# A selective scan with a shared feed-forward network: joined slot order, tanh gates, row shift on GpSimd, logits copied by ScalarE

## The chip, the cores and the metric

The kernel runs on 1 core of one Trainium2 chip. The metric is the device time of one execution in microseconds (us), the median of several runs; lower is better.

## What is computed

Two residual blocks on `x` of 4 x 512 tokens with 512 features. The first is a selective scan (Mamba's cross form: the context goes in, the normalised `x` is the gate `z`); the second is a mixture of 16 experts of which each token takes two, beside one shared expert of twice the width that every token takes.

```python
x = x + xattn(ctx, layernorm(x))            # first block
#   u = silu(conv(ctx @ in_proj)); dt, B, C from u
#   state = state * exp(dt * A) + (dt * u) * B ; y = sum_n state * C
#   y = (y + D * u) * silu(z)
n = layernorm(x)
logits = n @ gate_w.T ; top 2 of softmax    # routing, 16 experts
x = x + sum over the 2 experts (silu(g) * u) @ w_down * weight
      + (silu(g_s) * u_s) @ shared_down     # shared expert, 2 x 352 wide
```

## The kernel before, in words

The program is written out by hand for five engines, each with its own list of instructions, and semaphores between them. It has four stages: a prelude that makes `u`, `dt`, `B`, `C` and `silu(z)` for each of the 4 batches and stores them; the scan; a stretch that finishes the shared expert and computes the routing tables; and the routed experts.

**The scan stage** has 16 slots, one for each batch `b` and quarter `q` of the 512 channels. A slot has 16 steps `n`, one for each state. In a step ScalarE makes the decay `exp(dt * A)` in one of three PSUM banks (`decay`, L838), VectorE scans it with `dbu` (`scan`, L1226), and the result times `C` is made by VectorE (`times_c`, L1237, 12 states, tile `gs`, a ring of six) or by GpSimd (`times_c`, L1057, states 1, 5, 9 and 13, tile `g_p`, a ring of two). GpSimd makes `dbu` for four states at a time (L1043) for the slot after the one that VectorE scans: a group can be written when the scan has left it. TensorE adds the products up turned, in the bank `Y` (`y_sum`, L546, in the order `ORDER`).

**Between these steps lies the shared expert.** While batch `b` is scanned, slot `(b, q)` also treats tile `j = (b-1)*4+q` of 128 tokens of the batch before, and the next one. The constants at L41 to L51 say after which step `n` each piece of it stands on its engine. On TensorE `slot` (L625) takes ten early pieces of the next tile (`PE_AT`: eight halves of the four products of `rows_in`, L600, each two matrix products of 352 columns, then two turns, L608), six late pieces of the present tile (`LATE_AT`: the down projection, L618, each one product of 512 columns), the router (L579, into the first 16 columns of bank `YO`) and the turn of the normalised rows (L571). ScalarE applies the gate (`gate`, L851, Silu of a 128x352 half `c`), copies the turned hidden rows (`hT_copy`, L856 and L857), makes the normalised rows (`xn`, L863) and copies them turned (`xnT_copy`, L868). VectorE makes the hidden rows (`hidden`, L1276, gate times up), the statistics (`stats`, L1256 to L1261), the row shift minus mean times `rstd` (`norm`, L1266), copies the logits out of `YO` (`lg_copy`, L1270) and adds the down product to the rows (`add_shared`, L1281). GpSimd only raises the variance to the power of -1/2 (`rstd`, L1061).

The waits that matter: the second product into a gate's bank waits for `sg_ready` (the gate has been read); `hidden` waits for the gate and for the up product; the first down piece waits until the logits have left `YO`; `add_shared` waits for the last down piece; TensorE's first early piece of a slot waits for `hT_copy`. The scan stage is followed by `whole` for the tiles that are left, and by the routing in VectorE's list (L1347 to L1427).

The constants that set the places before:

```python
RSTD_AFTER = 2
LATE_AT = (0, 0, 0, 0, 0, 2, 3, 4, 4, 4, 6, 6, 6, 6, 6, 6, 6)
XN_TURN_AT, ROUTER_AT = (12, 9), 1
TAKE_AT, LOGITS_AT, GATED_AT, HIDDEN_AT, STATS_AT, NORM_AT, ADD_AT = 2, 4, 4, (12, 15), (10, 1), (12, 5), 13
```

## Time and profile before

| what | value |
|---|---|
| time, median of 3 runs (lowest to highest) | 1181.41 us (1180.92 to 1182.24) |
| the profiled execution: its own time | 1183.43 us |
| its span | 1181.7 us |
| busy: TensorE, VectorE, ScalarE, GpSimd | 937.7, 851.1, 534.8, 717.6 us |
| granted TensorE clock, mean | 0.877 of full speed |
| scan stage, from the first scan to the last product read | 166.9 to 701 us |
| from there to the last routing table | 701 to 798 us |
| routed experts | from 798 us |

The durations below are from the profiled execution, whose own time lies 2.0 us above the median. The shares of busy time are means over stages with different limits; the rows are therefore read inside one slot.

### The profile page before, as it was taken

The numbers are of one execution on the slowest core, as the hardware profiler recorded it, in microseconds if no ns is written. First come the engines' busy times: TensorE is split into PE (matmuls) and PEld (weight loads), VectorE is DVE, ScalarE is ACT, GpSimd is POOL, SyncE is SP. The second block draws the span as 40 slices with busy tenths as digits, with TensorE's granted clock in tenths as the row PEclk, the third lists the DMA queues.
The fourth block names the chain that finished last, engine by engine and source line by source line (L and its number), as shares of the span: only waits on it lengthen the run. The fifth ranks groups of instructions, "written<-read, shape, count | busy, mean of one in ns | idle before, by whom it ended". The sixth has DMA issues, their size and how long they took to land.

```text
span 1181.7 us, 16742 instructions
## 1 busy us (share of the span) xinstructions
PE 937.7 (79%) x4328; PEld 677.0 (57%) x4329; DVE 851.1 (72%) x1398; ACT 534.8 (45%) x918; POOL 717.6 (61%) x445
## 2 busy tenths in 40 slices
PE   5777414667788887888778898996999899988993
PEld 1222103455455555555555555564999899887893
DVE  4467457998889878888799861377879888888200
ACT  3677623444445453554454432201455455443551
POOL 0222359997777766767677510001789788876783
PEclk9777656578899888889888898998999999999997
DMA  8637230155122732146222013003586776776332
GB/s 278 256 140 286 109 125 18 54 187 201 57 72 63 276 125 70 44 136 232 86 71 71 27 53 128 18 19 109 130 223 165 200 208 173 215 193 161 66 66 36
DMA packets 69589, 152.03 MB, mean 129 GB/s; under 512 B 7200, under 2 KB 23584, under 8 KB 63920
## 3 DMA queue, kind: packets, MB, share of 16 engines
q1 hardware_dynamic: 59024, 126.97, 30.9%
q0 software_dynamic: 10528, 24.65, 11.4%
q8 instruction: 13, 0.21, 0.1%
q14 instruction: 24, 0.20, 0.1%
HBM read 112.80 MB, written 38.80 MB: 128 GB/s over the span
## 4 chain that ended last, share of the span: by engine, by line
DVE 27%; PE 25%; issue 15%; DMA 8%; ACT 5%; POOL 4%; DVEq 1%; ACTq 0%; SPq 0%; POOLq 0%
PE bank L600 10%; DMA e_gu<-in_wgu 6%; DVE e_gu_lo L1454 5%; DVE gs L1237 5%; DVE e_gu_hi L1453 4%; DVE bank L1226 4%; PE bank L618 4%; PE bank L546 3%; DVE bank L1446 3%; POOL dbu L1043 2%; PE bank L697 2%; PE bank L699 2%; PE bank L698 2%; ACT bank L838 1%; ACT L851 1%
## 5 line engine op out<-in xcount | busy, mean ns | idle before, releaser
L1043 POOL TENSOR_TENSOR dbu<-bcs,m_w 128x2048 f32<-128x2048 f32 x64 | 295.4, 4621 | 75.8 <-DVE bank L1226 75.8
L838 ACT ACTIVATE bank<-m_dt,c_a 128x512 f32<-128x512 f32 x256 | 171.3, 686 | 271.6 <-DVE gs L1237 271.5
L1226 DVE TENSOR_TENSOR_SCAN bank<-bank,dbu 128x512 f32<-128x512 f32 x192 | 230.7, 1219 | 30.4 <-ACT bank L838 21.6
L600 PE MATMUL bank<-ws_gu,f_xnT 128*128 128x352 f32 x576 | 219.2, 526 | 38.5 <-ACT f_hT L857 35.7
L546 PE MATMUL bank<-ident,gs 128*128 128x128 f32 x768 | 136.3, 314 | 104.0 <-DVE gs L1237 98.3
L546 PEld LDWEIGHTS bank<-ident,gs 128*128 128x128 f32 x768 | 102.9, 163 | 151.0 <-DVE gs L1237 94.1
L600 PEld LDWEIGHTS bank<-ws_gu,f_xnT 128*128 128x128 f32 x576 | 116.5, 215 | 98.5 <-ACT f_hT L857 39.1
L697 PE MATMUL bank<-e_gu_hi,e_xT_hi 128*128 x376 | 130.1, 346 | 10.8 <-DVEq L1465 10.7
L1237 DVE TENSOR_TENSOR gs<-bank,bcs 128x512 f32<-128x512 f32 x192 | 128.3, 669 | 0.0
L699 PE MATMUL bank<-e_gu_hi,e_xT_lo 128*128 x376 | 122.4, 326 | 0.0
L698 PE MATMUL bank<-e_gu_lo,e_xT_hi 128*128 x376 | 122.4, 326 | 0.0
L618 PE MATMUL bank<-ws_dn,f_hT 128*128 128x512 f32 (+1 forms) x216 | 108.1, 624 | 0.0
L1057 POOL TENSOR_TENSOR g_p<-h_p,bcs 128x512 f32<-128x512 f32 x64 | 81.6, 1275 | 37.3 <-DVE h_p L1226 33.3
L1089 POOL TENSOR_TENSOR e_xT_lo<-e_xT,e_xT_hi 128x512 fp32r<-128x512 f32 x47 | 84.8, 1805 | 23.8 <-ACT e_xT_hi L938 23.8
L1084 POOL DMA_INDIRECT e_x<-xn_scratch,t_tok x47 | 47.2, 1004 | 72.7 <-DVE t_w L1427 65.1
L1106 POOL DMA_INDIRECT out_rows<-e_y,t_tok x47 | 75.0, 1596 | 25.4 <-DMA out_rows<-e_y,t_tok 12.5
L1446 DVE CAST bank<-e_gu 128x352 fp32r<-128x352 f32 x128 | 63.8, 522 | 32.0 <-DMA e_gu<-in_wgu 26.2
L1226 DVE TENSOR_TENSOR_SCAN h_p<-bank,dbu 128x512 f32<-128x512 f32 x64 | 77.4, 1209 | 3.1 <-POOL g_p L1057 3.1
L697 PEld LDWEIGHTS bank<-e_gu_hi,e_xT_hi 128*128 128x128 f32 x376 | 71.5, 190 | 12.9 <-issue 12.9
L965 ACT ACTIVATE e_y<-bank,zero,t_w 128x512 f32<-128x512 f32 x47 | 36.7, 780 | 85.8 <-PE bank L699 84.2
L698 PEld LDWEIGHTS bank<-e_gu_lo,e_xT_hi 128*128 128x128 f32 x376 | 71.8, 191 | 0.0
L699 PEld LDWEIGHTS bank<-e_gu_hi,e_xT_lo 128*128 128x128 f32 x376 | 71.6, 190 | 0.0
(163 smaller groups left out, 1668.6 us busy)
## 6 DMA issues: line engine op xcount, KB each, us to landing
bcs<-bc_scratch SPq DMA_DIRECT2D x32, 1024.0 KB, 8.8
e_gu<-in_wgu SPq DMA_DIRECT2D x16, 1408.0 KB, 6.9
e_dn<-in_wdn SPq DMA_DIRECT2D x16, 512.0 KB
out_rows<-xt SPq DMA_DIRECT2D x18, 256.0 KB, 2.1
p_x<-in_x SPq DMA_DIRECT2D x4, 1024.0 KB, 6.4
u_scratch<-p_u SPq DMA_DIRECT2D x4, 1024.0 KB, 3.9
silu_z_scratch<-p_sz SPq DMA_DIRECT2D x4, 1024.0 KB, 8.3
dt_scratch<-p_dt SPq DMA_DIRECT2D x4, 1024.0 KB, 3.9
```

The lines of the kernel that those rows point to most:

```text
L546: last = mm(Y[:, t * P:(t + 1) * P], tile[:, t * P:(t + 1) * P], ident[:], is_transpose=True, start=first and t == 0, stop=final and t == ...
L600: last = mm(dst[:, 0:I], lhs[t], ws_gu[:, t, off:off + I], start=t == 0, stop=t == KH - 1)
L618: last = mm(YO[:], f_hT[0:n, c, t, :], ws_dn[0:n, c, t, :], start=c == 0 and t == 0, stop=c == 1 and t == 2)
L697: mm(dst, a_hi, w_hi, start=first, stop=False)
L698: mm(dst, a_hi, w_lo, start=False, stop=False)
L699: return mm(dst, a_lo, w_hi, start=False, stop=final)
L838: f(HS[k % RING_H][:], m_dt[:, q % 2, :], ACT.Exp, scale=c_a[:, q, n:n + 1]).then_inc(exp_done, 1)
L1043: g.tensor_tensor(part_, Bs[:, gr * GRP:(gr + 1) * GRP, :], w, ALU.mult).then_inc(dbu_ready, 1)
L1089: g.tensor_tensor(e_xT_lo[:, par, :], e_xT[:], e_xT_hi[:, par, :].bitcast(F32), ALU.subtract).then_inc(xT_split, 1)
L1226: v.tensor_tensor_scan(to, h, dbu[:, n, :], 0.0, ALU.mult, ALU.add).then_inc(scan_done, 1)
L1237: v.tensor_tensor(gs[:, (q * NV + at) % RING_G, :], HS[k % RING_H][:], Cs[:, n, :], ALU.mult).then_inc(g_ready, 1)
L1446: v.tensor_copy(ROUNDED[(at + j) % 3][0:n, 0:w].bitcast(F32R), raw[0:n, t, c:c + w]).then_inc(rounded_done, 1)
```

## The change

It joins four edits in the same places.

1. The gate. Silu of a half is no longer one ACTIVATE. ScalarE computes `tanh(g/2)` into `f_sg` and `g/2` into a new tile `f_g` (then signals `sg_ready`), waits for its own result and adds 1 to `f_sg` (signal `raised`). GpSimd multiplies the two (`swish`, signal `swish_ready`), and `hidden` waits for that. The value is the same: g/2 * (1 + tanh(g/2)) = silu(g).
2. The row shift `f_nm` is made by GpSimd, directly behind the power, no more by VectorE.
3. ScalarE copies the logits, after step 5; VectorE did so after step 4.
4. The order: the router stands at the start of TensorE's slot, no more behind step 1; the six down pieces stand one by one behind steps 5 to 10, no more in four groups behind steps 4, 5, 6 and 9; `add_shared` stands after step 14 (13 before); `stats` of the first quarter after step 8 (10), its power after GpSimd's group 1 (2).

```diff
-RSTD_AFTER = 2
+RSTD_AFTER = 1
+SWISH_AFTER = 1
-LATE_AT = (0, 0, 0, 0, 0, 2, 3, 4, 4, 4, 6, 6, 6, 6, 6, 6, 6)
-XN_TURN_AT, ROUTER_AT = (12, 9), 1
+LATE_AT = (0, 0, 0, 0, 0, 0, 1, 2, 3, 4, 5, 6, 6, 6, 6, 6, 6)
+XN_TURN_AT = (12, 9)
-TAKE_AT, LOGITS_AT, GATED_AT, HIDDEN_AT, STATS_AT, NORM_AT, ADD_AT = 2, 4, 4, (12, 15), (10, 1), (12, 5), 13
+TAKE_AT, LOGITS_AT, GATED_AT, HIDDEN_AT, STATS_AT, ADD_AT = 2, 5, 4, (12, 15), (8, 1), 14
...
+                if rows:
+                    router(f, f[0], f[0])
                 for piece in early[0:PE_AT[0]] + late[0:LATE_AT[0]]:
                     piece()
...
-                    if rows and n == ROUTER_AT:
-                        router(f, f[0], f[0])
...
             def gate(fx, c):
                 act.wait_ge(gate_ready, 2 * fx[0] + c + 1)
                 act.wait_ge(h_ready, 1 + 2 * fx[0])
-                f(f_sg[:, c, :], GU[c][:, 0:I], ACT.Silu).then_inc(sg_ready, 1)
+                f(f_sg[:, c, :], GU[c][:, 0:I], ACT.Tanh, scale=0.5)
+                f(f_g[:, c, :], GU[c][:, 0:I], ACT.Copy, scale=0.5).then_inc(sg_ready, 1)
+                act.wait_ge(sg_ready, 2 * fx[0] + c + 1)
+                f(f_sg[:, c, :], f_sg[:, c, :], ACT.Identity, bias=1.0).then_inc(raised, 1)
...
+            def lg_copy(fx):
+                act.wait_ge(lg_ready, fx[0] + 1)
+                f(logits[:, bass.ds(fx[0], 1), :].rearrange("p a e -> p (a e)"), LG, ACT.Copy).then_inc(lg_copied, 1)
...
                     decay(b, q, n)
+                    if rows and n == LOGITS_AT:
+                        lg_copy(j)
...
             xn_of(3)
+            lg_copy((first + 2, 2))
             whole((first + 2, 2))
...
                     g.tensor_tensor(part_, Bs[:, gr * GRP:(gr + 1) * GRP, :], w, ALU.mult).then_inc(dbu_ready, 1)
+                    if rows and gr == SWISH_AFTER:
+                        swish(((b - 1) * DT + q, q))
...
+            def swish(f):
+                for c in range(2):
+                    pool.wait_ge(raised, 2 * f[0] + c + 1)
+                    g.tensor_tensor(f_sg[:, c, :], f_sg[:, c, :], f_g[:, c, :], ALU.mult).then_inc(swish_ready, 1)
...
             def rstd(j):
                 pool.wait_ge(var_ready, j[0] + 1)
-                g.tensor_tensor(f_rs[:, j[1]:j[1] + 1], f_ve[:, j[1]:j[1] + 1], halves[:, 0:1], ALU.pow).then_inc(rstd_ready, 1)
+                at = j[1]
+                g.tensor_tensor(f_rs[:, at:at + 1], f_ve[:, at:at + 1], halves[:, 0:1], ALU.pow).then_inc(rstd_ready, 1)
+                pool.wait_ge(rstd_ready, j[0] + 1)
+                held(pool)
+                g.tensor_scalar(f_nm[:, at:at + 1], f_mv[:, at, 0:1], f_rs[:, at:at + 1], -1.0, ALU.mult, ALU.mult).then_inc(norm_ready, 1)
...
-            for q in range(TB):
-                rstd((NT - TB + q, q))
+            for q in range(TB - 1):
+                rstd((first + q, q))
+            swish((first + 1, 1))
+            rstd((NT - 1, TB - 1))
+            for f in range(first + 2, NT + 2):
+                swish((f, f % TB))
...
-            def norm(j):
-                at = j[1]
-                dve.wait_ge(rstd_ready, j[0] + 1)
-                v.scalar_tensor_tensor(f_nm[:, at:at + 1], f_mv[:, at, 0:1], -1.0, f_rs[:, at:at + 1], ALU.mult, ALU.mult).then_inc(norm_ready, 1)
...
             def hidden(f, c):
-                dve.wait_ge(sg_ready, 2 * f[0] + c + 1)
+                dve.wait_ge(swish_ready, 2 * f[0] + c + 1)
                 dve.wait_ge(up_ready, 2 * f[0] + c + 1)
```

**TensorE, slot `q = 1`, steps 5 to 8** (L618 and L620 are the down pieces, L600 and L602 the early pieces, L546 and L548 the sums of `y`). Before, from the sum behind step 4 on:

```order
L546 MATMUL bank<-ident,gs 128x128 x4
L616 REGISTER_ALU
L618 MATMUL bank<-ws_dn,f_hT 128x512 x2
L562 REGISTER_ALU
L546 MATMUL bank<-ident,gs 128x128 x4
L618 MATMUL bank<-ws_dn,f_hT 128x512
L562 REGISTER_ALU
L546 MATMUL bank<-ident,gs 128x128 x4
L600 MATMUL bank<-ws_gu,f_xnT 128x352 x2
L618 MATMUL bank<-ws_dn,f_hT 128x512
```

With the change, from the sum behind step 5 on:

```order
L548 MATMUL bank<-ident,gs 128x128 x4
L618 REGISTER_ALU
L620 MATMUL bank<-ws_dn,f_hT 128x512
L564 REGISTER_ALU
L548 MATMUL bank<-ident,gs 128x128 x4
L602 MATMUL bank<-ws_gu,f_xnT 128x352 x2
L620 MATMUL bank<-ws_dn,f_hT 128x512
L561 REGISTER_ALU
L548 MATMUL bank<-ident,g_p 128x128 x4
L620 MATMUL bank<-ws_dn,f_hT 128x512
L558 REGISTER_ALU
L548 MATMUL bank<-ident,m_du 128x128 x4
```

One down piece instead of three now stands ahead of the early piece of step 6, and the last one stands behind step 10 instead of 9.

**ScalarE, slot `q = 1`, the gates between steps 9 and 10** (the bank is a decay). Before:

```order
L838 ACTIVATE bank<-m_dt,c_a 128x512
L849 ISA
L851 ACT_TABLE_LOAD
L851 ACTIVATE f_sg<-bank 128x352
L849 REGISTER_ALU
L851 ACTIVATE f_sg<-bank 128x352
L835 REGISTER_ALU
L838 ACT_TABLE_LOAD
L838 ACTIVATE bank<-m_dt,c_a 128x512
```

With the change:

```order
L840 ACTIVATE bank<-m_dt,c_a 128x512
L851 ISA
L853 ACTIVATE f_sg<-bank 128x352
L854 ACTIVATE f_g<-bank 128x352
L856 ACTIVATE f_sg<-f_sg 128x352
L851 REGISTER_ALU
L853 ACTIVATE f_sg<-bank 128x352
L854 ACTIVATE f_g<-bank 128x352
L856 ACTIVATE f_sg<-f_sg 128x352
L837 REGISTER_ALU
L840 ACTIVATE bank<-m_dt,c_a 128x512
```

Both table loads are gone, and four ACTIVATEs have come.

**GpSimd, slot `q = 1`, behind group 1.** With the change (before, the product for state 9 followed `dbu` directly):

```order
L1059 TENSOR_TENSOR dbu<-bcs,m_w 128x2048
L1080 ISA
L1081 TENSOR_TENSOR f_sg<-f_sg,f_g 128x352
L1080 REGISTER_ALU
L1081 TENSOR_TENSOR f_sg<-f_sg,f_g 128x352
L1086 TENSOR_TENSOR f_rs<-f_ve,halves 128x1
L1089 TENSOR_SCALAR f_nm<-f_mv,f_rs 128x1
L1070 REGISTER_ALU
L1075 TENSOR_TENSOR g_p<-h_p,bcs 128x512
```

The two gate products, and in this slot the power and the shift of the first quarter, stand in front of the product for state 9.

## Rows read from the trace of the kernel before

**Rows 1.** VectorE's waits, 286 to 700 us: total us, times, longest.
```profile
DVE bank L1226 <- ACT bank L838: 19.3, 14, 1.5
DVE logits L1270 <- PE bank L579: 18.1, 12, 3.5
DVE f_h L1276 <- issue: 12.0, 12, 1.6
DVE f_nm L1266 <- POOL f_rs L1061: 5.9, 3, 2.1
```

**Rows 2.** Timeline of VectorE, one slot: start, us, instruction, idle before it.
```profile
501.19 0.17 DVE L1270 COPY logits<-bank 128x16 f32 x1 [0.92 <-PE bank L579]
...
503.08 0.87 DVE L1266 SCALAR_TENSOR_TENSOR f_nm<-f_mv,f_rs 128x1 f32<-128x1 f32 x1
...
506.12 0.67 DVE L1237 TENSOR_TENSOR gs<-bank,bcs 128x512 f32<-128x512 f32 x1
...
511.68 2.55 DVE L1226 TENSOR_TENSOR_SCAN bank<-bank,dbu 128x512 f32<-128x512 f32 x2 [1.47 <-ACT bank L838]
...
517.98 0.52 DVE L1276 TENSOR_TENSOR f_h<-f_sg,bank 128x352 f32<-128x352 f32 x1 [1.45 <-issue]
...
520.16 0.69 DVE L1281 TENSOR_TENSOR xt<-xt,bank 128x512 f32<-128x512 f32 x1
```

**Rows 3.** Timeline of VectorE, first and last row of twelve slots, one shift.
```profile
285.16 0.67 DVE L1244 TENSOR_TENSOR bank<-bank,m_szT 128x512 f32<-128x512 f32 x1
...
310.53 0.16 DVE L1266 SCALAR_TENSOR_TENSOR f_nm<-f_mv,f_rs 128x1 f32<-128x1 f32 x1 [1.64 <-POOL f_rs L1061]
...
700.48 0.70 DVE L1244 TENSOR_TENSOR bank<-bank,m_szT 128x512 f32<-128x512 f32 x1 [1.51 <-PE bank L546]
```

**Rows 4.** Timeline of TensorE, the same slot.
```profile
504.60 1.88 PE L618 MATMUL bank<-ws_dn,f_hT 128*128 128x512 f32 x4
...
514.87 0.66 PE L546 MATMUL bank<-ident,gs 128*128 128x128 f32 x4 [1.91 <-DVE gs L1237]
515.36 2.52 PE L600 MATMUL bank<-ws_gu,f_xnT 128*128 128x352 f32 x4
...
520.39 0.60 PE L546 MATMUL bank<-ident,gs 128*128 128x128 f32 x4
520.83 2.53 PE L600 MATMUL bank<-ws_gu,f_xnT 128*128 128x352 f32 x8
523.20 0.60 PE L546 MATMUL bank<-ident,g_p 128*128 128x128 f32 x4
...
529.38 2.71 PE L600 MATMUL bank<-ws_gu,f_xnT 128*128 128x352 f32 x4 [2.88 <-ACT f_hT L857]
```

**Rows 5.** Timeline of ScalarE, the gates of that slot.
```profile
507.53 1.28 ACT L851 ACT_TABLE_LOAD   x1
508.83 0.82 ACT L851 ACTIVATE f_sg<-bank 128x352 f32<-128x352 f32 x2
509.66 1.28 ACT L838 ACT_TABLE_LOAD   x1
```

**Rows 6.** Groups by line, whole span: xcount | busy us, mean ns.
```profile
L811 ACT ACTIVATE p_ln<-p_e 128x512 f32<-128x512 f32 x16 | 8.8, 617 | 0.0
...
L1096 POOL TENSOR_TENSOR e_h<-e_sg,e_u 128x352 f32<-128x352 f32 x47 | 44.6, 948 | 14.7 <-issue 12.0 <-ACT e_u L948 2.4
```

**Rows 7.** Windows: us, busy PE, PEld, DVE, ACT, POOL, granted clock, DMA.
```profile
515.00:519.00 4.00, 4.00 (x10) 2.35 (x11) 2.55 (x4) 1.23 (x2) 3.94 (x1) 0.57 0.00 0
...
501.36:535.51 34.15, 28.59 (x133) 18.93 (x131) 30.06 (x40) 16.87 (x27) 25.12 (x11) 0.90 0.48 172
```

**Rows 8.** Timeline of GpSimd, the same slot.
```profile
502.67 1.27 POOL L1057 TENSOR_TENSOR g_p<-h_p,bcs 128x512 f32<-128x512 f32 x1 [0.20 <-DVE h_p L1226]
...
514.31 4.62 POOL L1043 TENSOR_TENSOR dbu<-bcs,m_w 128x2048 f32<-128x2048 f32 x1 [2.17 <-DVE bank L1226]
```

**Rows 9.** Timeline of TensorE, after the scan stage.
```profile
711.88 5.00 PE L600 MATMUL bank<-ws_gu,f_xnT 128*128 128x352 f32 x16 [1.09 <-ACT f_sg L851]
```

More of the change, by code:

```diff
@@ L169, in program @@
         f_sg = sb("f_sg", [P, 2, I])
+        f_g = sb("f_g", [P, 2, I])
         f_h = sb("f_h", [P, 2, I])
@@ L254, in program @@
             xt0_loaded xt1_loaded xt2_loaded xt3_loaded var_ready rstd_ready norm_ready xn_ready xn0_stored xn1_stored xnT_ready xnT_copied lg_ready lg_copied
-            gate_ready up_ready sg_ready h_ready hT_ready hT_copied down_ready down_added out_stored
+            gate_ready up_ready sg_ready raised swish_ready h_ready hT_ready hT_copied down_ready down_added out_stored
             trash_stored rt_max rt_exp rt_mask rt_rank rt_oh rt_table tables_ready
@@ L274, in program @@
          xt0_loaded, xt1_loaded, xt2_loaded, xt3_loaded, var_ready, rstd_ready, norm_ready, xn_ready, xn0_stored, xn1_stored, xnT_ready, xnT_copied, lg_ready,
-         lg_copied, gate_ready, up_ready, sg_ready, h_ready, hT_ready, hT_copied, down_ready, down_added,
+         lg_copied, gate_ready, up_ready, sg_ready, raised, swish_ready, h_ready, hT_ready, hT_copied, down_ready, down_added,
          out_stored, trash_stored, rt_max, rt_exp, rt_mask, rt_rank, rt_oh, rt_table,
-         tables_ready) = [s[n] for n in names[at:at + 42]]
+         tables_ready) = [s[n] for n in names[at:at + 44]]
         xt_loaded = [xt0_loaded, xt1_loaded, xt2_loaded, xt3_loaded]
@@ L771, in _ @@
             f = nc.scalar.activation
-            for count in (sz_ready, xd_copied, xnT_copied, hT_copied):
+            for count in (sz_ready, xd_copied, xnT_copied, hT_copied, lg_copied):
                 from_one(act, count)
@@ L916, in _ @@
             xn_of(1)
+            lg_copy((first, 0))
             xnT_of(1)
             xn_of(2)
+            lg_copy((first + 1, 1))
             xnT_of(2)
             xn_of(3)
+            lg_copy((first + 2, 2))
             whole((first + 2, 2))
             xnT_of(3)
+            lg_copy((NT - 1, TB - 1))
+            lg_copy((NT, 0))
             act.wait_ge(rt_max, 1)
@@ L1067, in _ @@
                     slot(b, q, True)
+            first = NT - TB
             for n in POOL_N:
+                if n == POOL_N[SWISH_AFTER + 1]:
+                    swish((first, 0))
                 times_c(B - 1, DT - 1, n)
-            for q in range(TB):
-                rstd((NT - TB + q, q))
+            for q in range(TB - 1):
[4 more added lines that the diff above has]
+                swish((f, f % TB))
             pool.wait_ge(tables_ready, 1)
@@ L1133, in _ @@
             v = nc.vector
-            for count in (dt_ready, h_ready, down_added, lg_copied, ey_taken):
+            for count in (dt_ready, h_ready, down_added, ey_taken):
                 from_one(dve, count)
@@ L1261, in stats @@
                 v.tensor_scalar(f_ve[:, at:at + 1], f_mv[:, at, 1:2], EPS, None, ALU.add).then_inc(var_ready, 1)
-            def norm(j):
-                at = j[1]
-                dve.wait_ge(rstd_ready, j[0] + 1)
-                v.scalar_tensor_tensor(f_nm[:, at:at + 1], f_mv[:, at, 0:1], -1.0, f_rs[:, at:at + 1], ALU.mult, ALU.mult).then_inc(norm_ready, 1)
-            def lg_copy(f):
-                dve.wait_ge(lg_ready, f[0] + 1)
-                v.tensor_copy(logits[:, bass.ds(f[0], 1), :].rearrange("p a e -> p (a e)"), LG).then_inc(lg_copied, 1)
             def hidden(f, c):
-                dve.wait_ge(sg_ready, 2 * f[0] + c + 1)
+                dve.wait_ge(swish_ready, 2 * f[0] + c + 1)
                 dve.wait_ge(up_ready, 2 * f[0] + c + 1)
@@ L1301, in slot @@
                     if rows:
-                        if n == LOGITS_AT:
-                            lg_copy(j)
                         if n == ADD_AT:
@@ L1307, in slot @@
                             stats(j, b - 1)
-                        if n == NORM_AT[q > 0]:
-                            norm(j)
                 times_c(b, q, NS - 1)
@@ L1328, in _ @@
                 stats((first + q, q), B - 1)
-                norm((first + q, q))
             whole((first + 1, 1))
-            for q in range(TB - 1):
-                lg_copy((first + q, q))
             stats((NT - 1, TB - 1), B - 1)
-            norm((NT - 1, TB - 1))
             whole((first + 2, 2))
-            lg_copy((NT - 1, TB - 1))
-            lg_copy((NT, 0))
             done = [0]
```

## The prediction

> **What bounds the kernel now.** The profiled execution took 1183.4 us, 2.0 above the median of 1181.4. The change touches only the slots that also carry the shared expert, and the tail behind them. So I read first VectorE's waits in those slots, then one slot on each engine in order of time. Twelve slots lie between the two reads of `Y` at 285.16 and 700.48 [rows 3]: 415.3 us. VectorE is their clock: in a slot of 34.15 us it works 30.06, GpSimd 25.12, ScalarE 16.87; TensorE is busy 28.59, but at a clock of 0.90 in the mean [rows 7]. What VectorE waits for is listed: 19.3 us for a decay, 18.1 for the router, 12.0 at `hidden`, 5.9 for the power [rows 1], 55 us in all.
>
> In the slot at 501 us I anchor everything at S, the end of VectorE's product of step 6, 506.12 + 0.67 = 506.79 [rows 2]. VectorE's idle time there is 0.92 before the logits, 1.47 before scan 10 and 1.45 before `hidden`; `add_shared` starts at 520.16, S + 13.4, without a wait [rows 2]. The "issue" before `hidden` is really TensorE: its up piece starts at 515.36 and takes 2.52 us, to 517.88 [rows 4], and `hidden` starts at 517.98 [rows 2].
>
> **The change, part by part, for such a slot.**
>
> *Logits off VectorE:* the 0.92 wait and 0.17 of work go [rows 2]: 1.1. ScalarE has the copy instead, 16 columns where half of 0.82 us buys 352 [rows 5], behind a router that now stands at the slot's start. ScalarE idles half the slot [rows 7], so I count nothing; without that cover one decay a slot would be late by at most 0.4.
>
> *Shift off VectorE:* 0.87 of work goes, 0.8 without its overlap with the next instruction [rows 2]. The same instruction took 0.16 elsewhere [rows 3]; at 503.08 a GpSimd product was running since 502.67 for 1.27 [rows 8], and both ended at 503.94. GpSimd gets it, for between 0.1 and 0.9 us; it stands at the end of GpSimd's slot, and nobody needs it for another third of a slot, so nothing is counted.
> The Trainium skill (GPSIMD Engine Reference, Key points) says that GpSimd shares its SBUF interfaces with VectorE and contends with VectorE instructions that have two SBUF inputs. The shift is such an instruction, and the trace agrees, 0.87 against 0.16. By that rule GpSimd's new work would hold no other instruction of the slot, since each reads at most one tensor from SBUF.
>
> *Gates:* between two decays ScalarE needs 1.28 + 0.82 + 1.28 = 3.4 us now [rows 5]. Afterwards, for each half: Tanh and Copy, 0.82 together, as two Silus are, and the Identity, between 0.42 (617 ns for 512 columns [rows 6], in proportion) and 0.62; I take 0.48. Twice 1.3 is 2.6, so decay 10 comes 0.8 earlier, and some 0.6 of the 1.47 remains. In the trace the first Silu starts 0.02 behind the end of its load [rows 5].
> The Trainium skill (ScalarE: Activation LUTs, What ACT_TABLE_LOAD costs) adds a drain of 1.38 us to each switch of tables. By it the old block would be 6.1 us and the gain 3.5; the trace has no room for that drain.
>
> *GpSimd's gate products:* 0.95 each [rows 6], 1.9 a slot. GpSimd would work 25.1 + 1.9 + 0.3 = 27.3 of 32 us. They stand before the product for state 9 and group 2 of `dbu`, in front of which GpSimd idled 2.17 [rows 8]; that gap takes them. Group 1 starts when scan 7 is done, shortly before S, and takes 4.6 like group 2 [rows 8]; so the first gate product is out by S + 5.2 and the second by S + 6.1, and VectorE asks for the first at about S + 9. Nothing, then. If GpSimd were 4 us later, `hidden` would wait, and scan 13 and everything of VectorE behind it too.
>
> *TensorE's new order* decides. Prices from rows at full clock: a sum 520.83 - 520.39 = 0.44, an early piece (523.20 - 520.83)/2 = 1.19, a down piece 1.88/2, with overlap 0.9 [rows 4]. From the product of step 7 (S + 1.8) to the last down piece TensorE now issues without a gap: 7 sums and turns (3.1), 4 early pieces (4.8) and 5 down pieces (4.5), 12.4 us. So `add_shared` can start at S + 14.2. VectorE would be there at about S + 12.5, and waits **1.7 us, a new wait**. What TensorE gains: its 1.91 us of idle time at 514.87 [rows 4] is filled, and I expect the fall of the clock to 0.57 in 515 to 519 [rows 7] to go with it. Then the up piece takes 1.2 and not 2.52, and the wait at `hidden` shrinks from 1.45 to about 0.25.
> From `add_shared` to the next S the slot had 34.15 - 13.4 = 20.75 us. Less 1.1 and 0.8, and less scan 14 (1.13, half of the pair of 2.55 less overlap [rows 2]), which now stands ahead: 17.7. The slot is 14.2 + 17.7 = 31.9, **2.2 less**.
>
> *The sum.* Nine slots with q over 0: 9 x 2.2 = 19.8. `hidden` waited 1.0 in the mean [rows 1] and 1.45 here, so some slots were shorter already; between 0 and 12 x 0.45 = 5.4 I take 1.5 off: 18.3. Three first slots of a batch: of the router's 18.1 they have what nine times 0.92 leaves, 9.8, and all 5.9 of the power [rows 1], with 3 x (0.17 + 0.16) of work and 3 x 1.47 before scan 10: 21.1. There the statistics stand later, so VectorE is 1.1 sooner at step 7, while TensorE starts each slot at half clock (2.71 us for one piece at 529.38 [rows 4]) and stays late. I let 1.9 each come back at `hidden` and `add_shared`, between 0 and the full 3.3 a slot of the router's wait: 15.4. The last slot of the first batch has the gates alone: 0.9. Together 34.6.
> *The tail.* TensorE idled 1.09 for a Silu behind a table load [rows 9]; Tanh and Copy are 0.9 sooner than load and Silu. One later gate ends a chain, and there the extra Copy and a logits copy cost 0.5. GpSimd's last gate products now stand ahead of its first gather, and that ahead of a turn in TensorE's list; behind it TensorE waits for VectorE's first expert split anyway. Nothing, at most 1.9. Net 0.4.
> 1183.4 - 35.0 = 1148.4; on the median's scale **1146.4 us**.
>
> **The rivals.**
> *A. VectorE alone sets the slot.* If the late down pieces find more room than I give them, the slot is 34.15 - 1.9 - 1.47 - 1.45 + 0.6 = 29.9: 2.0 less than mine in twelve slots, 1122 us. For it: TensorE's busy time [rows 7] has room. Against: 12.4 us of work stand in one piece.
> *B. Something small stays late in each slot,* about 1.1 us: a part of the low clock, ScalarE or GpSimd. The slot is 33.0, the time 1159 us. For it: the clock fell at 515 and at 529. Against: before those falls TensorE idled 1.91 and 2.88 us [rows 4], and before the long piece it idles no more.
> *C. Slower.* Place: TensorE between step 7 and `add_shared`. At 1.2 GHz each microsecond of full-clock work there costs another. The gain of 2.2 is gone when 2.2 us of the 12.4 run so, 4.4 us of time; with 3.2 us of it the slot is 35.2, and the time 1193 us. For it: 4 us at 0.57 stand in that place now [rows 7]. Against: as in B.
> *D. The gates don't save their loads*, were Tanh in another table than Exp. Then 2.6 us come back into ScalarE's block, sum 9 waits for it, and `add_shared` is 2.1 later each time: 1171 us. For it: the trace has no Tanh. Against: the compiled order has no load in the slots.
>
> **How the numbers follow.** Forecast 0.62, A 0.13, B 0.17, C 0.05, D 0.03. The forecast's own ends are 1138 (down pieces at 0.86, nothing comes back in the first slots) and 1155 (the full 3.3 and the 5.4 there). The range has to take part of A and most of B: 1128 to 1164; the lower half of A, C and D are left out. A measurement here tells 0.2%, 2.4 us, from no change. Faster 0.93, same 0.02, slower 0.05.
>
> **What would show it.** Right: VectorE's rows of logits and shift gone; no table load between 286 us and the routed experts; a wait before scan 10 near 0.6; a new wait of VectorE for the down product (L620) at `add_shared`, about 1.7 each time; granted clock 1.00 where 0.57 stood; 382 us between the first and the last read of `Y`. Wrong: no wait at `add_shared` (A), a clock under 0.9 between step 7 and step 10 (B, C), or a wait of VectorE for GpSimd's gate product (L1081), which I have at none.

## The result, and the profile after

The changed kernel takes **1149.97 us** (median of 4 runs, 1147.77 to 1150.49) against 1181.83 for the kernel before beside it; the ratio is 0.972, 95% interval 0.9692 to 0.9747. The forecast was 1146.4. One execution of a kernel below (the shift put back) took 1274.3 us at a granted clock of 0.70 and is left out of its row. The profiled execution took 1150.49 us, its span is 1148.7 (1181.7 before): 33.0 less. I cut both spans at the fourth and the last read of `Y` [rows 3]:

| stretch | before | after | difference | forecast |
|---|---|---|---|---|
| start to the fourth read | 285.16 | 279.44 | -5.7 | -0.9 |
| fourth to last read, twelve slots | 415.32 | 383.05 | **-32.3** | -33.7 |
| last read to the end | 481.2 | 486.2 | **+5.0** | -0.4 |

VectorE's waits between the two reads, after (total us, times, longest), to be held against [rows 1]:

```profile
DVE xt L1307 <- PE bank L620: 16.9, 12, 1.5
DVE f_h L1302 <- issue: 5.7, 12, 0.5
DVE bank L1261 <- ACT bank L840: 5.4, 11, 0.9
DVE f_st L1291 <- DMA xt<-x_scratch: 4.8, 3, 1.8
```

The router and the power are gone, the wait for decays fell from 19.3 to 5.4 and that at `hidden` from 12.0 to 5.7. At the top stands a wait that was 0.4 us before: `add_shared` waits for the last down piece in each of the twelve slots. The last row was not foreseen: in the first quarter the statistics, now after step 8, are early for the load of their rows.

One slot of VectorE, against [rows 2]; the first and last row here are two reads of `Y`, the second row is the product of step 6:

```profile
473.42 0.67 DVE L1279 TENSOR_TENSOR bank<-bank,m_szT 128x512 f32<-128x512 f32 x1
...
481.99 0.67 DVE L1272 TENSOR_TENSOR gs<-bank,bcs 128x512 f32<-128x512 f32 x1
...
486.49 2.54 DVE L1261 TENSOR_TENSOR_SCAN bank<-bank,dbu 128x512 f32<-128x512 f32 x2 [0.41 <-ACT bank L840]
...
491.89 0.52 DVE L1302 TENSOR_TENSOR f_h<-f_sg,bank 128x352 f32<-128x352 f32 x1 [0.55 <-issue]
...
496.79 0.69 DVE L1307 TENSOR_TENSOR xt<-xt,bank 128x512 f32<-128x512 f32 x1 [1.53 <-PE bank L620]
...
505.26 0.67 DVE L1279 TENSOR_TENSOR bank<-bank,m_szT 128x512 f32<-128x512 f32 x1
```

S is 481.99 + 0.67 = 482.66. `add_shared` starts at S + 14.1 after a wait of 1.53, and the slot is 505.26 - 473.42 = 31.84 us (34.15 before, [rows 7]).

TensorE in the same slot, against [rows 4]: an early piece, the last down piece, and behind them the router and the first early piece of the next slot.

```profile
490.44 1.35 PE L602 MATMUL bank<-ws_gu,f_xnT 128*128 128x352 f32 x4
...
495.73 1.02 PE L620 MATMUL bank<-ws_dn,f_hT 96*128 96x512 f32 x2
...
502.54 1.73 PE L581 MATMUL bank<-c_gate,f_xnT 128*128 128x16 f32 x8
504.90 2.72 PE L602 MATMUL bank<-ws_gu,f_xnT 128*128 128x352 f32 x4 [0.63 <-ACT f_hT L862]
```

Windows of the same execution (columns as in [rows 7]): the slot, the place of the old fall, the start of the next slot.

```profile
473.42:505.26 31.84, 28.34 (x131) 19.78 (x130) 29.09 (x38) 15.91 (x31) 27.21 (x14) 0.88 0.30 92
484.00:497.00 13.00, 12.80 (x59) 8.23 (x59) 10.43 (x13) 7.49 (x14) 11.60 (x6) 1.00 0.04 14
502.00:508.00 6.00, 5.37 (x19) 4.15 (x18) 5.81 (x10) 2.52 (x7) 4.17 (x5) 0.50 0.95 363
```

From 484 to 497 TensorE works 12.8 of 13.0 us at full clock: the chain without a gap. The level of 1.2 GHz (0.50) has not gone in this slot, it stands at the slot's start. There it costs VectorE nothing: the slot just before this one ran at full clock throughout and is as long.

```profile
441.59:473.42 31.83, 25.41 (x131) 17.18 (x130) 29.08 (x38) 15.90 (x31) 27.23 (x15) 1.00 0.23 66
```

ScalarE and GpSimd in the same slot, against [rows 5] and [rows 8]:

```profile
483.32 0.44 ACT L853 ACTIVATE f_sg<-bank 128x352 f32<-128x352 f32 x1
483.67 0.45 ACT L854 ACTIVATE f_g<-bank 128x352 f32<-128x352 f32 x1
484.15 0.50 ACT L856 ACTIVATE f_sg<-f_sg 128x352 f32<-128x352 f32 x1
...
508.30 0.17 ACT L877 ACTIVATE logits<-bank 128x16 f32 x1
```

```profile
486.75 1.82 POOL L1081 TENSOR_TENSOR f_sg<-f_sg,f_g 128x352 f32<-128x352 f32 x2
...
505.00 0.27 POOL L1089 TENSOR_SCALAR f_nm<-f_mv,f_rs 128x1 f32<-128x1 f32 x1 [0.20 <-POOL f_rs L1086]
```

The two halves of the gate take 2.5 us in place of 3.4. The products are out at 488.57, 2.8 us before `hidden` asks (491.34).

**The 5.7 us at the start are not the change's.** The code there is the same. One group of products of the prelude shows what differs, before and after:

```profile
32.99 6.13 PE L534 MATMUL bank<-p_xd,p_dtw 16*128 16x512 f32 x8
```

```profile
33.18 3.70 PE L536 MATMUL bank<-p_xd,p_dtw 16*128 16x512 f32 x8
```

The granted clock was 0.59 in these 6.13 us and 1.00 in these 3.70. In four profiles of the fourteen of this study this group took 3.69 or 3.70 us, and their first scan starts at 160.7 to 161.6; in the others it took 5.0 to 6.6, and the first scan starts at 163.7 to 167.7. Kernels with the change's gates stand on both sides. So executions differ by up to 7 us before the scan begins. For that reason the runs below are compared by the stretch between the two reads first.

### The profile page after: what moved, and what is told of

The parts are those of the page before. It is cut to its first block, busy times and chain, and to the rows that moved or that the text cites. A ratio compares the mean times of both kernels' runs of the same rounds, so it can differ in the third digit from the quotient of the medians.

```text
span 1148.7 us, 16859 instructions
## 1 busy us (share of the span) xinstructions
PE 914.5 (80%) x4328; PEld 669.7 (58%) x4329; DVE 841.6 (73%) x1365; ACT 528.0 (46%) x979; POOL 752.8 (66%) x497
## 4 chain that ended last, share of the span: by engine, by line
PE 32%; DVE 28%; issue 14%; DMA 6%; POOL 4%; DVEq 2%; ACT 1%; SPq 0%; ACTq 0%; POOLq 0%
PE bank L602 8%; DVE bank L1261 8%; PE bank L620 7%; DVE gs L1272 4%; PE bank L548 4%; PE bank L699 4%; PE bank L701 3%; PE bank L700 3%; DVE e_gu_lo L1470 3%; DVE e_gu_hi L1469 3%; DMA e_gu<-in_wgu 3%; POOL dbu L1059 3%; DVE bank L1462 2%; DVE e_dn_lo L1470 1%; DVE h_p L1261 1%
## 5 line engine op out<-in xcount | busy, mean ns | idle before, releaser
L1261 DVE TENSOR_TENSOR_SCAN bank<-bank,dbu 128x512 f32<-128x512 f32 x192 | 231.6, 1220 | 15.4 <-POOL dbu L1059 8.0
L602 PE MATMUL bank<-ws_gu,f_xnT 128*128 128x352 f32 x576 | 203.5, 496 | 24.4 <-ACT f_hT L862 23.3
L548 PE MATMUL bank<-ident,gs 128*128 128x128 f32 x768 | 136.9, 312 | 106.2 <-DVE gs L1272 102.4
L548 PEld LDWEIGHTS bank<-ident,gs 128*128 128x128 f32 x768 | 101.9, 160 | 157.0 <-DVE gs L1272 97.8
L602 PEld LDWEIGHTS bank<-ws_gu,f_xnT 128*128 128x128 f32 x576 | 111.3, 206 | 75.3 <-ACT f_hT L862 24.5
L620 PE MATMUL bank<-ws_dn,f_hT 128*128 128x512 f32 (+1 forms) x216 | 110.3, 616 | 0.0
L1124 POOL TENSOR_TENSOR e_xT_lo<-e_xT,e_xT_hi 128x512 fp32r<-128x512 f32 x47 | 84.9, 1805 | 18.3 <-ACT e_xT_hi L954 18.3
L1075 POOL TENSOR_TENSOR g_p<-h_p,bcs 128x512 f32<-128x512 f32 x64 | 82.4, 1287 | 13.8 <-DVE h_p L1261 10.1
L1081 POOL TENSOR_TENSOR f_sg<-f_sg,f_g 128x352 f32<-128x352 f32 x36 | 33.3, 945 | 75.4 <-ACT f_sg L856 75.4
L699 PEld LDWEIGHTS bank<-e_gu_hi,e_xT_hi 128*128 128x128 f32 x376 | 70.7, 188 | 14.1 <-issue 14.1
```

Of the source, the lines that this page charges most:

```text
L548: last = mm(Y[:, t * P:(t + 1) * P], tile[:, t * P:(t + 1) * P], ident[:], is_transpose=True, start=first and t == 0, stop=final and t == ...
L602: last = mm(dst[:, 0:I], lhs[t], ws_gu[:, t, off:off + I], start=t == 0, stop=t == KH - 1)
L620: last = mm(YO[:], f_hT[0:n, c, t, :], ws_dn[0:n, c, t, :], start=c == 0 and t == 0, stop=c == 1 and t == 2)
L699: mm(dst, a_hi, w_hi, start=first, stop=False)
L1124: g.tensor_tensor(e_xT_lo[:, par, :], e_xT[:], e_xT_hi[:, par, :].bitcast(F32), ALU.subtract).then_inc(xT_split, 1)
L1261: v.tensor_tensor_scan(to, h, dbu[:, n, :], 0.0, ALU.mult, ALU.add).then_inc(scan_done, 1)
```

## The experiments

All runs in one table. "Stretch" is from the fourth to the last read of `Y` in the profile, "rest" from there to the span's end; the ratio is to the kernel before beside them.

| kernel | median (range) | ratio, 95% interval | stretch | rest |
|---|---|---|---|---|
| before | 1181.4 (1180.9 to 1182.2) | | 415.3 | 481.2 |
| after | 1150.0 (1147.8 to 1150.5) | 0.972, 0.9692 to 0.9747 | 383.1 | 486.2 |
| after, Silu gates | 1160.9 (1155.7 to 1165.4) | 0.981, 0.9766 to 0.9855 | 391.1 | 486.6 |
| after, shift on VectorE | 1164.2 (1163.2 to 1164.4) | 0.9853, 0.9827 to 0.9878 | 394.1 | 483.9 |
| after, logits on VectorE | 1151.2 (1149.5 to 1152.8) | 0.974, 0.9717 to 0.9763 | 383.4 | 484.4 |
| after, old places | 1137.6 (1134.8 to 1140.6) | 0.9635, 0.9611 to 0.9659 | 367.1 | 487.5 |
| after, old down pieces | **1132.7** (1132.1 to 1135.9) | 0.9586, 0.9543 to 0.963 | 363.5 | 482.9 |
| after, router behind step 1 | 1157.2 (1153.3 to 1159.3) | 0.9779, 0.9732 to 0.9826 | 389.0 | 486.3 |
| after, `ADD_AT` 15 | 1134.6 (1132.8 to 1136.3) | 0.96, 0.9557 to 0.9642 | 366.0 | 483.7 |
| old places, tail reordered | 1136.0 (1134.7 to 1137.9) | 0.9614, 0.9573 to 0.9655 | 366.7 | 486.5 |
| before, logits alone | 1169.8 (1167.8 to 1171.8) | 0.9885, 0.9827 to 0.9943 | 403.0 | 483.6 |
| before, gates alone | 1164.3 (1164.0 to 1169.7) | 0.9858, 0.9797 to 0.9919 | 397.3 | 486.1 |
| before, shift alone | 1170.5 (1165.8 to 1172.8) | 0.9886, 0.9824 to 0.9948 | 403.7 | 481.4 |
| after, GpSimd's gate work doubled | 1155.8 (1150.5 to 1158.6) | 0.9763, 0.97 to 0.9827 | 382.8 | 487.1 |

### One part undone

**Silu again.**

```diff
-                f(f_sg[:, c, :], GU[c][:, 0:I], ACT.Tanh, scale=0.5)
...
+                f(f_sg[:, c, :], GU[c][:, 0:I], ACT.Silu).then_inc(sg_ready, 1)
```

> The changed kernel with the gates made by Silu on ScalarE again (its two table loads back, the gate products of GpSimd gone); all else stays. Theory: in the slots ScalarE's block is 0.9 longer, so scan 10 comes 0.8 later, but VectorE had 1.5 us to spare before add_shared, and TensorE's list had only 0.4 to spare before the sum of step 10; so the add comes about 0.4 later in each of twelve slots, 5 us. Behind the scan stage the three gate chains lose GpSimd's product and win back some 2 to 3 us. Sum: 1152 to 1153 us. Rival: the gates give their whole 0.9 in each slot, and the stretch behind it is not theirs: 1160 or more. Second rival: the product on GpSimd costs more than the loads: under 1148.

Measured: 8.0 us more in the stretch. VectorE's timeline in one slot, and a line of its waits between the reads:

```profile
497.12 2.55 DVE L1255 TENSOR_TENSOR_SCAN bank<-bank,dbu 128x512 f32<-128x512 f32 x2 [1.47 <-ACT bank L840]
...
507.14 0.69 DVE L1301 TENSOR_TENSOR xt<-xt,bank 128x512 f32<-128x512 f32 x1 [1.53 <-PE bank L620]
```

```profile
DVE f_h L1296 <- issue: 3.3, 12, 0.3
```

Scan 10 waits 1.47 again, 1.06 more and not 0.8; and the wait at `add_shared` is still 1.53, so the down product moved with it, the whole 0.8 of the slot (32.63). TensorE had less to spare before the sum of step 10 than I said, and the rival with the full gate time was nearer (1160). That 2 to 3 us are won behind the scan stage did not show: the rest is 486.6. The last line matters for the account below: with the old gates, in the otherwise changed kernel, `hidden` waits no more than 0.3 a slot.

**The shift on VectorE again, after step 5.**

```diff
-                g.tensor_scalar(f_nm[:, at:at + 1], f_mv[:, at, 0:1], f_rs[:, at:at + 1], -1.0, ALU.mult, ALU.mult).then_inc(norm_ready, 1)
...
+                v.scalar_tensor_tensor(f_nm[:, at:at + 1], f_mv[:, at, 0:1], -1.0, f_rs[:, at:at + 1], ALU.mult, ALU.mult).then_inc(norm_ready, 1)
```

> The changed kernel with the row shift on VectorE again, after step 5 (after step 12 in the first quarter). Theory: 0.87 beside a running GpSimd product, 0.8 without overlap, in front of S, so all of it counts in nine slots: 7.2 us; nothing in the three first quarters, where it stands in front of the wait at add_shared. 1157 us. Rival: the time is absorbed by the new wait at add_shared (1.5 long): under 1152.

Measured: 11.1 us more in the stretch. Nine slots give 8.5 of it (7.2 said): what stands in front of S counts. Most of them are 32.3 us, half a microsecond more; two are 33.56 and 34.75. The three first quarters give 0.7 to 1.0 each, where nothing was expected: there the shift took 1.9 to 2.4 us beside GpSimd, and the wait at `add_shared` took in only a part of that (13.8 us in nine slots are left of 16.9 in twelve). VectorE and GpSimd in a slot of 32.31 us:

```profile
489.23 0.55 DVE L1298 SCALAR_TENSOR_TENSOR f_nm<-f_mv,f_rs 128x1 f32<-128x1 f32 x1
```

```profile
485.15 4.62 POOL L1059 TENSOR_TENSOR dbu<-bcs,m_w 128x2048 f32<-128x2048 f32 x1
```

The shift ends at 489.78 and GpSimd's instruction at 489.77, as both ended at one time in the kernel before (503.95 and 503.94, [rows 2, 8]). And in the slot of 34.75 us:

```profile
587.77 1.78 DVE L1298 SCALAR_TENSOR_TENSOR f_nm<-f_mv,f_rs 128x1 f32<-128x1 f32 x1
```

```profile
583.70 4.61 POOL L1059 TENSOR_TENSOR dbu<-bcs,m_w 128x2048 f32<-128x2048 f32 x1
588.20 1.33 POOL L1075 TENSOR_TENSOR g_p<-h_p,bcs 128x512 f32<-128x512 f32 x1
```

Here the shift was held by two products of GpSimd in a row, to 589.55 (the second ends at 589.53). The same happened in the slot of 33.56 us, 1.80 in place of 0.55; in that of 34.75 `hidden` waited 1.73 besides.

**The logits on VectorE again, after step 5**, the router still at the slot's start.

```diff
+                        if n == LOGITS_AT:
+                            lg_copy(j)
```

> The changed kernel with the logits copied by VectorE again, after step 5; the router stays at the slot's start. Theory: the router is done 5 us before VectorE asks, so nothing waits, and 0.17 of work a slot is left: 12 x 0.17 = 2 us; 1152 us (1150 to 1153). Rival: the place on VectorE itself cost the 0.92 (a wait in the slot, as before): 12 us, 1161.

Measured: 0.3 us in the stretch, 1.2 in the median. With the router early the copy may stand on either engine. Of this edit only the wait was worth money.

**The old places.**

```diff
-LATE_AT = (0, 0, 0, 0, 0, 0, 1, 2, 3, 4, 5, 6, 6, 6, 6, 6, 6)
+LATE_AT = (0, 0, 0, 0, 0, 2, 3, 4, 4, 4, 6, 6, 6, 6, 6, 6, 6)
-TAKE_AT, LOGITS_AT, GATED_AT, HIDDEN_AT, STATS_AT, ADD_AT = 2, 5, 4, (12, 15), (8, 1), 14
+TAKE_AT, LOGITS_AT, GATED_AT, HIDDEN_AT, STATS_AT, ADD_AT = 2, 5, 4, (12, 15), (10, 1), 13
```

(with `RSTD_AFTER` 2 and the router behind step 1; the logits stay after step 5 on ScalarE, since after step 4 ScalarE would wait there for the router, the router for the first early piece, and that for a copy of ScalarE that stands behind.)

> The changed kernel with the places of before: the down pieces in four groups behind steps 4, 5, 6 and 9, the router behind step 1, add_shared after step 13, the statistics of the first quarter after step 10. Gates, shift and logits stay as changed. Theory: the wait of 1.5 at add_shared is gone (VectorE comes to it at S + 12.5 and finds the sum ready), and scan 14 stands behind it, 1.13; against that TensorE idles before step 9 again, its clock falls to half there, and hidden waits 1.2. So the slot is 31.4 to 32.6, and the time between 1145 and 1159, 1152 as one number. Rival: the order carries the gain (TensorE's gap and clock): slots of 33 or more, 1164 or more. Rival the other way: the order costs 1.5 a slot: 1132.

Measured: **16.0 us less** in the stretch, 12.4 in the median: the order of the change costs, it doesn't pay. VectorE's timeline and the window of one slot (columns as in [rows 7]):

```profile
485.49 0.68 DVE L1307 TENSOR_TENSOR xt<-xt,bank 128x512 f32<-128x512 f32 x1
```

```profile
465.13:495.06 29.93, 25.13 (x131) 17.40 (x130) 28.97 (x37) 15.90 (x31) 27.20 (x14) 0.99 0.36 115
```

`add_shared` waits for nothing, the slot is 29.93 us of which VectorE works 28.97, and TensorE's mean clock is 0.99 in this slot. The second rival (a price of 1.5 a slot) was nearest.

### Which part of the order

**The down pieces alone put back.**

```diff
-LATE_AT = (0, 0, 0, 0, 0, 0, 1, 2, 3, 4, 5, 6, 6, 6, 6, 6, 6)
+LATE_AT = (0, 0, 0, 0, 0, 2, 3, 4, 4, 4, 6, 6, 6, 6, 6, 6, 6)
```

> The changed kernel with the down pieces alone in their old groups (behind steps 4, 5, 6 and 9); the router stays at the slot's start, add_shared after step 14. Theory, after the run with all places put back had slots of 29.9 us, a granted clock of 1.00 and no wait at add_shared: what cost 1.9 a slot is the last down pieces behind step 10. So the wait of 1.5 at add_shared is gone here, the slots are about 30.3, and the stretch from the fourth to the last read of Y falls from 383 to about 370; 1138 us (1135 to 1144). Rival: the router at the slot's start does it, since 1.73 us of it run at half clock ahead of the first early piece: the stretch stays at 380 or more, 1148. Second rival: the late place of the add.

**The router alone put back behind step 1.**

```diff
-                if rows:
-                    router(f, f[0], f[0])
...
+                    if rows and n == 1:
+                        router(f, f[0], f[0])
```

> The changed kernel with the router alone behind step 1 again; the down pieces stay one by one behind steps 5 to 10. Theory (down pieces): slots stay at 31.8, the wait of 1.5 at add_shared stays; 1150 (1147 to 1152). Rival (router): the slot starts at full clock, the wait at add_shared shrinks, slots near 30.5; 1138.

**`add_shared` after step 15.**

```diff
-TAKE_AT, LOGITS_AT, GATED_AT, HIDDEN_AT, STATS_AT, ADD_AT = 2, 5, 4, (12, 15), (8, 1), 14
+TAKE_AT, LOGITS_AT, GATED_AT, HIDDEN_AT, STATS_AT, ADD_AT = 2, 5, 4, (12, 15), (8, 1), 15
```

> The changed kernel with add_shared after step 15 in place of 14: scan 15, the product of 14 and hidden stand ahead of it, 2.2 us. Theory of the prediction: the wait at add_shared is VectorE against TensorE's chain of 12.4 us from step 7; moved behind 2.2 us of other work it is gone, the slot loses up to 1.5 us, 12 x 1.5 = 18 us at most: 1132 to 1138. Rival: TensorE is the limit of the whole slot and not only of that place (28.3 of 31.8 us busy, at a clock of 0.88): the wait comes back at another place, at the read of Y or hidden, and the time stays over 1144.

Measured: the old down pieces give 19.6 us of the stretch (13 were expected), and with 1132.7 us this kernel beats both before and after (0.985 of after's median); a later `add_shared` gives 17.1 (1134.6, inside what its theory gave); the router behind step 1 costs 5.9, which neither of its two expectations had. VectorE's waits between the reads with the old down pieces:

```profile
DVE bank L1261 <- ACT bank L840: 6.3, 14, 0.9
DVE f_st L1291 <- DMA xt<-x_scratch: 4.9, 3, 1.8
DVE f_h L1302 <- issue: 3.4, 12, 0.4
```

The 16.9 us at `add_shared` are gone, and nothing took their place. The first and the third run remove the same wait from its two sides, by an earlier writer and by a later reader, and agree within 2.5 us (`hidden` waits 5.7 in the third and 3.4 in the first): the wait is the price of the order. The window of a slot with the old down pieces and with `ADD_AT` 15:

```profile
470.18:500.11 29.93, 26.49 (x131) 18.35 (x131) 28.97 (x37) 15.91 (x31) 27.19 (x14) 0.95 0.33 97
```

```profile
468.15:498.35 30.20, 25.20 (x131) 17.20 (x130) 28.98 (x38) 15.91 (x31) 27.17 (x14) 1.00 0.26 71
```

The slot with the clock at 0.95 is the shorter one, and as short as that at 0.99 above: with the router at the start, TensorE's lower clock there is covered. With the router behind step 1, ScalarE waits for it in front of decays, and VectorE's wait for decays is 14.2 instead of 5.4. There the clock does count. The first 8 us of two slots of that run:

```profile
315.08:323.08 8.00, 8.00 (x31) 5.82 (x31) 6.57 (x10) 1.69 (x5) 7.74 (x5) 0.65 0.13 37
445.60:453.60 8.00, 7.08 (x39) 5.11 (x38) 8.00 (x11) 2.80 (x6) 7.75 (x5) 1.00 0.11 33
```

ScalarE's copy of the logits waited 3.91 us in the first and 2.10 in the second, and the slots are 33.37 and 31.84 us long. The router at the start is the part of the order that pays.

**The tail, on the kernel with the old places:** ScalarE makes the gates of the third tile before the rows of the fourth; the statistics of the first quarter after step 8.

```diff
-            xn_of(3)
             lg_copy((first + 2, 2))
             whole((first + 2, 2))
+            xn_of(3)
             xnT_of(3)
```

> All places put back as in the run before (1137.6 us), but the statistics of the first quarter after step 8, and behind the scan stage ScalarE makes the gates of the third tile and copies its turned rows ahead of the normalised rows of the fourth, which wait 9 us there for the store of earlier rows. Theory: the 9 us wait is then spent under the gates; some 8 of it are won between the last read of Y and the routing, where TensorE next needs 7 us for up, turns and down of that tile. The statistics give up to 3 x 1 us. 1137.6 - 8 - 1.5 = 1128 us. Rival: another wait on the same store, or VectorE's wait for the tile's load (5 us), takes its place: over 1134.

Measured: 1136.0 against 1137.6, the rest 486.5 against 487.5. ScalarE and TensorE there:

```profile
681.88 0.46 ACT L853 ACTIVATE f_sg<-bank 128x352 f32<-128x352 f32 x1 [4.63 <-PE bank L602]
```

```profile
676.87 12.07 PE L602 MATMUL bank<-ws_gu,f_xnT 128*128 128x352 f32 x32
```

The wait of 9 us was mostly covered: TensorE had the routers and then the gate products of that tile (the first part of the row above) to make in the same time, and the Tanh now waits for them. `hidden` of that tile came 40.2 us after the last read of `Y` instead of 42.4. The expectation of 8 us fell.

### One part alone, from before

The gates (with GpSimd's product behind group 1, as in the change):

```diff
-                f(f_sg[:, c, :], GU[c][:, 0:I], ACT.Silu).then_inc(sg_ready, 1)
+                f(f_sg[:, c, :], GU[c][:, 0:I], ACT.Tanh, scale=0.5)
...
-                dve.wait_ge(sg_ready, 2 * f[0] + c + 1)
+                dve.wait_ge(swish_ready, 2 * f[0] + c + 1)
```

> The kernel before with one edit: the gates by Tanh, Copy and Identity on ScalarE and a product on GpSimd. Theory of the prediction: the block is 0.8 to 0.9 shorter, no more: 12 x 0.85 = 10 us, and 1 lost behind the scan stage; 1172 us. Rival: the shorter gap of TensorE before step 9 (1.9 us before) keeps its clock at full there, as the slots of the run with all places put back suggest (clock 0.99 to 1.00): then the up piece takes 1.35 and not 2.52 and the wait at hidden goes too, 2 us a slot, 1160 or less. Rival the other way: GpSimd's product is late beside the old places, over 1178.

The logits:

```diff
+                    if rows and n == LOGITS_AT:
+                        lg_copy(j)
...
-                        if n == LOGITS_AT:
-                            lg_copy(j)
```

> The kernel before with one edit: ScalarE copies the logits (after step 5), VectorE no more; the router stays behind step 1. Theory, as in the sum of the prediction: 1.1 in each of nine slots, and in the three first quarters the 9.8 us of waits less what comes back: 14 us in all between the fourth and the last read of Y (415.3 before), 1167 to 1169 us. Rival 1: VectorE is handed more than it loses, because the clock of TensorE changes too: over 20 us, 1160 or less. Rival 2: ScalarE now waits for the router in front of decays that VectorE needs: under 8 us, 1174 or more.

The shift:

```diff
+                g.tensor_scalar(f_nm[:, at:at + 1], f_mv[:, at, 0:1], f_rs[:, at:at + 1], -1.0, ALU.mult, ALU.mult).then_inc(norm_ready, 1)
...
-                        if n == NORM_AT[q > 0]:
-                            norm(j)
```

> The kernel before with one edit: the row shift on GpSimd behind the power. Theory: 0.8 in each of nine slots, and in three first quarters the 5.9 us of waits for the power and 0.16 each, 13.6 us together; 1168 us. Rival: it comes back at the wait for the decay of step 10 or at hidden, since ScalarE and TensorE set those: under 5 us, 1177 or more.

Measured in the stretch: gates **18.1**, logits **12.3**, shift **11.6**, together 42.0; the three in one kernel (after with the old places) give 48.2. VectorE's waits between the reads with the gates alone, and with the logits alone:

```profile
DVE logits L1286 <- PE bank L581: 21.5, 12, 3.4
DVE bank L1247 <- ACT bank L840: 6.8, 14, 0.9
...
DVE f_h L1297 <- issue: 3.3, 12, 0.3
```

```profile
DVE bank L1252 <- ACT bank L840: 26.8, 18, 2.7
...
DVE f_h L1298 <- issue: 5.4, 12, 1.0
```

The gates take 12.5 off the wait for decays and 8.7 off `hidden`, though no down piece was moved, and give 3.4 back at the router: 17.8 of the 18.1. That is 1164.3 us where 1172 was expected; the rival on TensorE's clock (1160) was nearer. Logits and shift came out 2 us under the theory each. With the logits alone the 18.1 of the router went, 7.5 came as later decays (ScalarE waits for the router itself), and 6.6 went at `hidden`. But VectorE now comes to the shift earlier, while GpSimd still makes `dbu`: in seven of the nine slots the shift took 1.8 to 2.0 us in place of 0.9, over all twelve 14.9 us in place of 8.6. These 6.3 us go once the shift is on GpSimd too. They and the 3.4 and 3.1 that gates and shift, each alone, give back at the router are among the terms that make the three together 6.2 better than their sum, though the wait at `hidden` can be won only once.

### GpSimd's share

```diff
-                    g.tensor_tensor(f_sg[:, c, :], f_sg[:, c, :], f_g[:, c, :], ALU.mult).then_inc(swish_ready, 1)
+                    g.tensor_tensor(f_g[:, c, :], f_sg[:, c, :], f_g[:, c, :], ALU.mult).then_inc(extra, 1)
+                    pool.wait_ge(extra, 2 * f[0] + c + 1)
+                    g.tensor_tensor(f_sg[:, c, :], f_g[:, c, :], ones[:, 0:1].to_broadcast([P, I]), ALU.mult).then_inc(swish_ready, 1)
```

> The changed kernel with GpSimd's gate work doubled: each product is written to f_g first, and a second product (by one) moves it to f_sg; some 2.1 us more a slot, 29.3 of 31.8. Theory (GpSimd's share costs nothing in the slots): the products end at about S + 7.8, hidden asks at S + 9; the stretch between the reads stays within 2 us of 383; behind it three chains get 1.1 each: 1153 us (1150 to 1156). Rival: GpSimd is at its limit, dbu or the product for state 9 becomes late: 1 us a slot or more, 1163 or more.

GpSimd's and VectorE's timelines in one slot:

```profile
492.33 0.94 POOL L1081 TENSOR_TENSOR f_g<-f_sg,f_g 128x352 f32<-128x352 f32 x1
...
495.09 0.77 POOL L1083 TENSOR_TENSOR f_sg<-f_g,ones 128x352 f32<-128x352 f32 x1
```

```profile
497.45 0.52 DVE L1304 TENSOR_TENSOR f_h<-f_sg,bank 128x352 f32<-128x352 f32 x1 [0.54 <-issue]
```

The stretch is 382.8 us against 383.1: doubled, the work still costs nothing in the slots. The median lies 5.8 higher. In the profiles the span is 6.1 longer, of which 5.4 are the later fourth read (284.82 against 279.44), which is the prelude's, and 0.9 lie behind the last read.

## Why the prediction was right, and where its steps were not

**The limit, right.** The slot was worked out from S: down product at S + 14.2, VectorE there at S + 12.5, a wait of 1.7, a slot of 31.9. Measured: S + 14.1, S + 12.6, 1.5, 31.84. The new wait stands at `add_shared` in all twelve slots, `hidden` waits 0.55 (0.25 said), scan 10 waits 0.41 (0.6 said), there is no table load and no wait for L1081 in the slots (behind them there is one, see the tail). 383.05 us lie between the reads (382 said).

**What the order is worth: the step that failed.** The prediction let the new order fill TensorE's gap of 1.91 us and so take the low clock and the wait at `hidden` away, and counted its new wait as the price. The run with the gates alone shows that the gates do this with the old order: `hidden` falls from 12.0 to 3.3, TensorE's gap of 1.91 to 1.24, and its clock between 10.5 and 23.5 us behind each read of `Y` is 1.00 in all twelve slots, where before it was 0.87 to 0.94 in eight of them. With Silu put back in the changed kernel (new order, logits and shift moved) it is 3.3 again, and 1.00 in all twelve. So the wait can go without the gates and without the order, and beside the gates the order has nothing more to take there. The gates' term was 0.8 to 0.9 a slot; alone they give 18.1 us in twelve slots, 1.5 each in the mean, and beside the new order 8.0. What the order would be worth without them no run shows. Beside them only its new wait and the earlier router were left, and undoing the whole order gives 16.0. The sum came out right because it was made at the place that ends last, for the order as it stands; its parts were credited wrongly. What rival A says, 29.9 us a slot with VectorE alone, is what the kernel does once the down pieces are back (29.93). That A needed only one constant was not seen. (Rival C's 1193 is worked out from the kernel before; on the sum's own scale, 12 x 3.2 above the forecast, it is about 1185. Nothing hung on it.)

**Logits and shift, right in kind.** 12.3 and 11.6 alone, where the same terms from the same rows gave 14 and 13.6. The prediction gave the shift a fixed price of 0.8; what it costs is the rest of one or two GpSimd products, 0.5 to 2.4 us by the place where VectorE meets them. GpSimd's products cost nothing in the slots, as said, and doubled neither.

**First quarters, over-rated.** The three first slots went from 112.7 to 100.1 us, 12.6 less and not 15.4. The wait for the rows' load, 1.6 us each, is a new one behind the earlier statistics; it was not among the steps. The nine others gave 19.6 (18.3 said). The last slot of the first batch gave nothing (30.45 and 30.42 us) and not 0.9: `hidden` waits 1.79 there instead of 0.77.

**The tail, wrong in sign.** Forecast 0.4 less, measured 5.0 more, and only a part of it is explained. 4.8 of the 5.0 had come by VectorE's first row of the routed experts, 97.9 us behind the last read of `Y` before and 102.7 after. In the fourteen profiles the rest varies between 481.2 and 487.5, and with Silu put back it is 486.6 as well. What the rows show: TensorE's first down pieces there took 6.37 us where they took 5.42, and later ones 6.84 where they took 5.32, at a clock of 0.83 and 0.78 where it was 1.00. VectorE waited 7.4 us for the load of its rows where it had waited 0.5. And the gate chains wait for GpSimd's product, which the prediction had named as a sign of being wrong:

```profile
DVE f_h L1302 <- POOL f_sg L1081: 16.1, 3, 13.0
```

Little of the 16.1 is new: `hidden` waited 15.7 us there before, all of it for TensorE, and 20.2 now, with 4.1 for TensorE. Last, the products hold VectorE's small routing instructions up. Before, VectorE:

```profile
760.96 0.18 DVE L1362 CAST r_ixf<-r_ix 128x32 f32<-128x32 uint32 x1
...
776.85 0.17 DVE L1388 TENSOR_TENSOR r_base<-r_end,r_nt 128x16 f32<-128x16 f32 x1
```

After, VectorE and GpSimd:

```profile
724.77 0.70 DVE L1378 CAST r_ixf<-r_ix 128x32 f32<-128x32 uint32 x1
...
741.44 0.90 DVE L1404 TENSOR_TENSOR r_base<-r_end,r_nt 128x16 f32<-128x16 f32 x1
```

```profile
724.50 0.93 POOL L1081 TENSOR_TENSOR f_sg<-f_sg,f_g 128x352 f32<-128x352 f32 x1 [19.43 <-ACT f_sg L856]
...
741.27 1.04 POOL L1081 TENSOR_TENSOR f_sg<-f_sg,f_g 128x352 f32<-128x352 f32 x1 [13.42 <-ACT f_sg L856]
```

Both ends agree to 0.04 us: 725.47 and 725.43, 742.34 and 742.31. With a third such row (0.42 before, 1.03 after; it ends 0.28 behind GpSimd's) the rows are 1.9 us longer. What that costs can be read: from VectorE's copy of the totals (L1389) to its cast at L1423 it is 9.33 us before (there L1373 to L1407) and in the three kernels without GpSimd's product (Silu put back, logits alone, shift alone), and 10.7 to 11.1 in the ten with it. So 1.3 of the 5.0 us are the product's; the rest stays open. The prediction asked only for the slots whether GpSimd's new work would hold VectorE.

**The clock.** Full where 0.57 stood, as said; that this slot's mean would still be 0.88 (router and first early piece at 0.50) was not. Over the twelve slots the mean goes from 0.88 to 1.00, and their lengths don't follow it.
